# Four residual layers with chosen weights on one core: where the sync queue reads the ids

## The chip, the cores and the metric

The kernel runs on one core of a Trainium2 chip. The metric is the device time of one execution in microseconds (us), as the median of several runs. Five engines work side by side: TensorE (PE in the profile), VectorE (DVE), ScalarE (ACT), GpSimd (POOL) and SyncE (SP). SP computes nothing here. It waits, forms addresses and issues nearly all transfers, which 16 DMA engines then carry out.

## The reference, cut to what matters

Eight sequences of 128 tokens with 512 features pass through four layers, each added to its input. The layers choose weights by one id per sequence:

```python
def reference(x, itok_B_0_15, itok_B_0_7, itok_B_0_4, itok_B_2_6, ...):
    x = x + _L0_cond_ref(x, itok_B_0_15, L0_cond_weight)
    x = x + _L1_cond_ref(x, itok_B_0_7, L1_cond_W, L1_cond_Wr, L1_cond_A, L1_cond_B)
    x = x + _L2_cond_ref(x, L2_cond_weight, L2_cond_bias, L2_cond_lora_A, L2_cond_lora_B, itok_B_0_4)
    x = x + _L3_cond_ref(x, ..., itok_B_2_6, 0)
    return x

def _L0_cond_ref(x, adapter_ids, weight):
    w = weight[adapter_ids]                    # (8, 512, 512), one matrix for each sequence
    return jnp.einsum('bsi,boi->bso', x, w)
```

Layer 1 is a dense product with a router over eight small experts, to which a language id adds a bias. Layer 2 is a dense product with a low-rank part whose first factor is chosen by an id. Layer 3 is a gated feed-forward block of width 1376 with three low-rank parts, all chosen by an id. Everything is float32.

## The kernel before, in words

Each engine has a program of its own, written out by hand, and semaphores join them. There is no planner: the order of the work is the order of the lines in each engine's block.

**Layer 0** goes sequence by sequence (b = 0 to 7). Each sequence has its own 1 MB matrix, which SP fetches into a ring of three buffers (`w0_raw`, `W0_RING = 3`). The matrix of sequence 0 comes as four transfers of 256 KB (L367), and TensorE multiplies them directly as float32 (L1185). The matrix of every later sequence comes as three transfers of 512, 256 and 256 KB (L378). TensorE uses the first quarter directly (L1188). For the other three quarters ScalarE makes a rounded high part (L498, called at L533), VectorE the remainder (L749, called at L806), and TensorE takes three products of each (L1196 to L1198). ScalarE also copies the result of the sequence before out of PSUM (L510), TensorE transposes it (L1146), and VectorE adds it to x (L761). From sequence 3 on, TensorE also does layer 1's thin product with the router's weights (L1166).

**The sync queue** is the one that the change touches. In order of its lines it does this:

- It reads the eight ids of layer 0 into registers (L364). The helper `ids_of` (L356) does this with two instructions, both on L358: one reads the address of the array of ids, one reads the ids.
- It issues the four transfers of sequence 0 (L367).
- For b = 1 to 7 it issues x of the sequence (L371, from b = 2 on; x of sequences 0 and 1 is issued by ScalarE's queue), waits for a free buffer (L373, or L375 and L376 from b = 4 on) and issues the three transfers of the matrix (L378). Behind b = 2 it issues the router's weights and the language ids (L384, L385). Behind b = 3 (`b == W0_RING`) it reads the ids of layers 2 and 3 (L381, L382).
- It issues the weights of layer 1 (L388, four transfers, and L389).
- It waits until the splits of sequence 6 are done (L391, L392), then issues the weights of layer 2 (L393, and L395 with the ids of layer 2).
- It waits until layer 0 is done (L399, L400), then issues the masks and layer 3's first low-rank factors (L401, and L403 with the ids of layer 3), and later all else of layer 3.

The order around the change, in the code:

```python
if b > W0_RING:
    sp.wait_ge(w0_raw_used, b - W0_RING)
    sp.wait_ge(w0_lo, KC * (b - W0_RING))
```

Layers 1 to 3 work on halves of four sequences. Their products need no ids from SP other than through the transfers named above.

Of the kernel before, what the change touches and what calls it, by code (L numbers as in the profile page):

```python
# [37 lines left out]
B, S, D = 8, 128, 512  # L38
# [17 lines left out]
W0_RING = 3  # L56
# [5 lines left out]
def bass_four_residual_layers(nc, xT, ids0, ids1, ids2, ids3, w0, w1, aw1, b1, w2, a2, b2, bias2,  # L62
                              wgu, agu, sel, bgu, wd, ad, bd, out):
    ctx = ExitStack()
    with ctx:
# [188 lines left out]
        def x_f_tokens(o, cols):  # L254

            return x_f[:, cols.start // S:cols.stop // S, o]
# [51 lines left out]
        def chunks_of(n):  # L308

            return 2 * (n // 2) + 1, 2 * (n // 2) + 2  # L310

        def raw_slot(fc):
            return 0 if fc == 0 else (fc - 1) % 4 ^ 2
# [5 lines left out]
        def bgu_count(n, i):  # L319

            return 1 + 2 * n + i + 1
# [31 lines left out]

        @block.sync
        def _(sp):
            def ids_of(src, last):  # L356

                _, ids = nc.values_load_multi_w_load_instructions(  # L358
                    src[0:1, 0:B], engines=[mybir.EngineType.SP], min_val=0, max_val=last,
                    skip_runtime_bounds_check_because="each id only forms the DRAM address of a transfer, "  # L360
                                                      "and the transfer checks that address itself")
                return ids

            adapter0 = ids_of(ids0, w0.shape[0] - 1)  # L364

            for c in range(C):
                sp.dma_start(w0_raw[0][:, c], w0[adapter0[0]][:, c * D:(c + 1) * D]).then_inc(w0c_in[c], 16)  # L367
            for b in range(1, B):
                adapter = adapter0[b]
                if b >= 2:  # L370
                    sp.dma_start(x_f[:, b], xT[b]).then_inc(x_in[b], 16)  # L371
                if b == W0_RING:
                    sp.wait_ge(l0_tm, 1)  # L373
# [3 lines that stand above are left out]
                for k, (first, end) in enumerate(((0, 2), (2, 3), (3, 4))):  # L377
                    sp.dma_start(w0_raw[b % W0_RING][:, first:end],  # L378
                                 w0[adapter][:, first * D:end * D]).then_inc(w0_in[b % W0_RING][k], 16)
                if b == W0_RING:  # L380
                    adapter2 = ids_of(ids2, a2.shape[0] - 1)  # L381
                    adapter3 = ids_of(ids3, agu.shape[0] - 1)  # L382
                if b == 2:
                    sp.dma_start(aw1_raw[:], aw1).then_inc(aw1_in, 16)  # L384
                    sp.dma_start(lang_i[:], ids1.partition_broadcast(P)).then_inc(lang_in, 16)  # L385

            for o in range(C):
                sp.dma_start(w1_raw[:, o], w1[:, o]).then_inc(w1_in[o], 16)  # L388
            sp.dma_start(b1_raw[:], b1).then_inc(b1_in, 16)  # L389

            sp.wait_ge(w0_raw_used, 6)  # L391
            sp.wait_ge(w0_lo, KC * 6)  # L392
            sp.dma_start(w2_raw[:], w2).then_inc(w2_in, 16)  # L393
            for b in range(B):
                sp.dma_start(a2_raw[:, b], a2[adapter2[b]]).then_inc(a2_in, 16)  # L395
            sp.dma_start(b2_raw[:], b2).then_inc(b2_in, 16)
            sp.dma_start(bias_sb[:], bias2).then_inc(bias_in, 16)

            sp.wait_ge(l0_tm, 8)  # L399
            sp.wait_ge(l0_tr, 8)  # L400
            sp.dma_start(sel_raw[:], sel).then_inc(sel_in, 16)  # L401
            for b in range(B):
                sp.dma_start(agu_raw[:, b], agu[adapter3[b]]).then_inc(agu_in, 16)  # L403

            def load_wgu(fc):
                sp.dma_start(wgu_raw[raw_slot(fc)][:], wgu[fc]).then_inc(wgu_in[raw_slot(fc)], 16)

            def load_bgu(p):

                f1, f2 = chunks_of(2 * p)  # L410
                for b in range(B):
                    rows = slice(64 * (b % 2), 64 * (b % 2) + 64)
                    sp.dma_start(bgu_raw[rows, :, b // 2],  # L413
                                 bgu[adapter3[b], f1:f2 + 1].rearrange("f r n -> r f n")).then_inc(bgu_in, 16)

            sp.wait_ge(w12_lo, nth["w2_3"])
            load_wgu(0)
            for b in range(B):
                rows = slice(64 * (b % 2), 64 * (b % 2) + 64)
                sp.dma_start(bgu_raw[rows, 1, b // 2], bgu[adapter3[b], 0]).then_inc(bgu_in, 16)  # L420
            load_wgu(1)
            load_wgu(2)
            sp.wait_ge(l2_tm, 2)
            for b in range(B):
                sp.dma_start(ad_raw[:, b], ad[adapter3[b]]).then_inc(ad_in, 16)
            sp.wait_ge(wgu_lo, 1)
            sp.wait_ge(bgu_ready, 1)
            sp.wait_ge(main_done, 16)
            load_bgu(0)
            load_wgu(3)  # L430
            load_wgu(4)
            for p in range(1, PAIRS):
                sp.wait_ge(bgu_ready, bgu_count(2 * p - 1, 1))
                load_bgu(p)
                if p + 1 < PAIRS:
                    sp.wait_ge(wc_lo, 3 * 2 * p)
                    load_wgu(2 * p + 3)
                    load_wgu(2 * p + 4)
            sp.wait_ge(bgu_ready, bgu_count(2 * PAIRS - 1, 1))
            sp.wait_ge(wc_lo, 3 * 2 * PAIRS)  # L440
            for o in range(C):
                sp.dma_start(wd_raw[:, o], wd[o]).then_inc(wd_in[o], 16)
            sp.wait_ge(c22_ready, 2 * PAIRS)
            for b in range(B):
                rows = slice(64 * (b % 2), 64 * (b % 2) + 64)
                sp.dma_start(bd_raw[rows, b // 2], bd[adapter3[b]]).then_inc(bd_in, 16)
            for i, (o, cols) in enumerate(DOWN_PIECES):
                sp.wait_ge(x3_sum, i + 1)
                sp.dma_start(out[o, :, cols].rearrange("p (b s) -> p b s", s=S), x_f_tokens(o, cols)).then_inc(out_sent, 16)
            sp.wait_ge(out_sent, 16 * len(DOWN_PIECES))  # L450
# [1099 lines left out]
```

## Time and profile before

| | |
|---|---|
| median of 3 runs | 303.03 us (303.0 to 304.06) |
| the profiled execution's own time | 302.71 us |
| its span in the trace | 300.9 us |
| TensorE busy | 290.3 us, 96% of the span |
| VectorE, ScalarE, GpSimd busy | 204.4, 142.4 and 10.7 us |
| granted TensorE clock, mean | 0.997 |
| moved by DMA | 33.29 MB, 111 GB/s over the span |

The span is the time from the first to the last instruction of the program. The profiled execution took 1.8 us more than its span. A busy TensorE is not a TensorE at its peak, since the ends of its instructions are modelled and consecutive ones overlap. Times of rows are counted from the start of the span.

### The profile page before, as it was taken

How to read it: one execution, taken by the hardware profiler on the slowest of the kernel's cores; microseconds unless marked ns; L12 is line 12 of the kernel's file. 1: busy time of each engine (PE TensorE's matmuls, PEld its weight loads, DVE VectorE, ACT ScalarE, POOL GpSimd, SP SyncE). 2: the span in 40 equal slices, each digit the busy share in tenths (PEclk: the TensorE clock that was granted, in tenths of full speed). 3: DMA queues.
4: the chain of work that ended last, by engine and by line, in shares of the span. 5: the costliest groups of instructions: out<-in, count | busy, mean ns of one | idle time of the engine just before them, and what ended most of it. 6: DMA issues, size and time to landing. Idle time of an engine off the chain costs nothing.

```text
span 300.9 us, 4565 instructions
## 1 busy us (share of the span) xinstructions
PE 290.3 (96%) x1630; PEld 237.4 (79%) x1630; DVE 204.4 (68%) x378; ACT 142.4 (47%) x250; POOL 10.7 (4%) x25
## 2 busy tenths in 40 slices
PE   6799999999999999999999999999999999999995
PEld 5357788888888777787878878878889888888884
DVE  1297898894758899676967968878747959242003
ACT  2376861512425356756556465564633874211000
POOL 1030000000700001000000000000000000000000
PEclk9999999999999999999999999999999999999998
DMA  5989993004404062006116026031075200022004
GB/s 179 340 298 321 396 322 106 0 0 133 148 0 99 0 184 99 0 20 219 42 46 232 3 60 222 0 87 53 2 288 170 70 1 0 0 72 70 0 2 139
DMA packets 23255, 33.29 MB, mean 111 GB/s; under 512 B 2624, under 2 KB 15424, under 8 KB 23104
## 3 DMA queue, kind: packets, MB, share of 16 engines
q1 hardware_dynamic: 22944, 32.47, 32.5%
q10 hardware_dynamic: 288, 0.52, 0.6%
q8 instruction: 13, 0.21, 0.3%
q14 instruction: 10, 0.08, 0.1%
HBM read 30.89 MB, written 2.10 MB: 110 GB/s over the span
## 4 chain that ended last, share of the span: by engine, by line
PE 64%; DVE 13%; SPq 7%; DMA 6%; issue 4%; ACT 4%; DVEq 0%; ACTq 0%
PE bank L1212 11%; PE bank L1213 11%; PE bank L1214 11%; PE bank L1342 6%; PE bank L1343 6%; PE bank L1344 6%; DMA w_raw<-in_w 4%; SPq L413 3%; SPq L358 3%; DMA bgu_raw<-in_bgu 2%; PE bank L1321 2%; PE bank L1166 2%; DVE bgu_st L924 2%; DVE part L1038 2%; PE bank L1416 2%
## 5 line engine op out<-in xcount | busy, mean ns | idle before, releaser
L1212 PE MATMUL bank<-act_hl,wd_hl 128*128 128x512 f32 (+1 forms) x99 | 36.5, 369 | 0.0
L498 ACT ACTIVATE part<-bank 128x512 f32<-128x512 f32 x40 | 23.7, 595 | 26.8 <-PE bank L1344 26.2
L1213 PE MATMUL bank<-act_hl,wd_hl 128*128 128x512 f32 (+1 forms) x99 | 36.3, 367 | 0.0
L1214 PE MATMUL bank<-act_hl,wd_hl 128*128 128x512 f32 (+1 forms) x99 | 36.2, 365 | 0.0
L1038 DVE TENSOR_TENSOR part<-bank,part 128x512 f32<-128x512 f32 x40 | 26.7, 685 | 5.1 <-PE bank L1321 3.8
L749 DVE TENSOR_TENSOR w_hl<-w_raw,w_hl 128x512 fp32r<-128x512 f32 x29 | 19.3, 695 | 10.0 <-ACT w_hl L498 10.0
L924 DVE SCALAR_TENSOR_TENSOR bgu_st<-bgu_st,lo_rows,bgu_raw 128x512 fp32r<-128x512 f32 (+1 forms) x21 | 15.4, 773 | 14.3 <-ACT bgu_st L498 14.3
L749 DVE TENSOR_TENSOR act_hl<-act_f,act_hl 128x512 fp32r<-128x512 f32 x22 | 14.9, 689 | 12.9 <-ACT act_hl L498 12.8
L498 ACT ACTIVATE act_hl<-act_f 128x512 fp32r<-128x512 f32 x22 | 13.6, 624 | 20.8 <-PE bank L1214 18.8
L498 ACT ACTIVATE w_hl<-w_raw 128x512 fp32r<-128x512 f32 x29 | 17.8, 625 | 11.4 <-DMA w_raw<-in_w 10.0
L1214 PEld LDWEIGHTS bank<-act_hl,wd_hl 128*128 128x128 f32 x99 | 18.6, 188 | 3.1
L1212 PEld LDWEIGHTS bank<-act_hl,wd_hl 128*128 128x128 f32 x99 | 18.7, 189 | 3.0 <-issue 0.2
L1213 PEld LDWEIGHTS bank<-act_hl,wd_hl 128*128 128x128 f32 x99 | 18.7, 189 | 2.7
L664 ACT ACTIVATE act_f<-part 128x512 f32<-128x512 f32 x20 | 12.5, 632 | 15.7 <-DVE part L1038 15.7
L1072 DVE TENSOR_TENSOR x_f<-bank,x_f 128x512 f32<-128x512 f32 (+1 forms) x9 | 5.5, 629 | 19.5 <-PE bank L1437 19.5
L498 ACT ACTIVATE xb<-x_f 128x512 fp32r<-128x512 f32 x16 | 10.0, 628 | 17.3 <-DVE x_f L869 13.2
L1321 PEld LDWEIGHTS bank<-t_st,bgu_st 128*128 128x128 f32 x88 | 14.7, 188 | 3.9 <-DVE t_st L1022 0.9
L1321 PE MATMUL bank<-t_st,bgu_st 128*128 128x256 f32 x88 | 15.8, 284 | 0.9 <-DVE t_st L1022 0.9
L1344 PE MATMUL bank<-xb,wc_gate 128*128 128x512 f32 x40 | 15.7, 394 | 0.0
L1343 PE MATMUL bank<-xb,wc_gate 128*128 128x512 f32 x40 | 15.7, 392 | 0.0
L1342 PE MATMUL bank<-xb,wc_up 128*128 128x512 f32 x40 | 15.6, 391 | 0.0
L1343 PE MATMUL bank<-xb,wc_up 128*128 128x512 f32 x40 | 15.6, 390 | 0.0
(172 smaller groups left out, 689.9 us busy)
## 6 DMA issues: line engine op xcount, KB each, us to landing
w_raw<-in_w SPq DMA_DIRECT2D x22, 256.0 KB, 7.3
wgu_raw<-in_wgu SPq DMA_DIRECT2D x11, 512.0 KB, 4.5
bgu_raw<-in_bgu SPq DMA_DIRECT2D x40, 128.0 KB, 2.7
w_raw<-in_w SPq DMA_DIRECT2D x7, 512.0 KB, 7.2
wd_raw<-in_wd SPq DMA_DIRECT2D x4, 704.0 KB, 6.0
out<-x_f SPq DMA_DIRECT2D x7, 256.0 KB, 2.4
x_f<-in_xT SPq DMA_DIRECT2D x6, 256.0 KB, 7.1
w_raw<-in_w SPq DMA_DIRECT2D x1, 1024.0 KB, 6.6
```

The lines of the kernel that those rows point to most:

```text
L498: return act.activation(dst, src, ACT.Copy)
L664: act.activation(act_f[:, fc, h * HT:(h + 1) * HT], part[0][C_PART[k]][:], ACT.Silu).then_inc(silu_done, 1)
L749: return dve.tensor_tensor(dst, src, hi.bitcast(F32), ALU.subtract)
L924: return dve.scalar_tensor_tensor(out=st, in0=st.bitcast(F32), scalar=lo_rows16[:, 0:1], in1=raw, op0=ALU.mult, op1=ALU.add)
L1038: dve.tensor_tensor(dst[:], bank[4 * (n % 2) + b][:], dst[:], ALU.add).then_inc(c_added, 1)
L1212: pe.matmul(dst, w_hi, x[0][:, cols], start=start, stop=False)
L1213: pe.matmul(dst, w_hi, x[1][:, cols], start=False, stop=False)
L1214: return pe.matmul(dst, w_lo, x[0][:, cols], start=False, stop=stop)
L1321: ins = pe.matmul(dst[:, q * 2 * S:(q + 1) * 2 * S], bgu_st[fc % 2][:, pair, g], t3_st[:, g, pair * 2 * S:(pair + 1) * 2 * S], start=False ...
L1342: pe.matmul(dst[:], hi, x[0][c], start=(start and c == 0), stop=False, skip_group_check=True)
L1343: pe.matmul(dst[:], hi, x[1][c], start=False, stop=False, skip_group_check=True)
L1344: ins = pe.matmul(dst[:], lo, x[0][c], start=False, stop=(stop and c == 1), skip_group_check=True)
```

## The change

The sync queue reads the id of sequence 0 alone, issues the four transfers of sequence 0, and then reads the other seven ids of layer 0 with a second call of the helper. The reads of the ids of layers 2 and 3 move from behind the transfers of sequence 3 to behind the last transfers of layer 1. Nothing else differs.

```diff
-            def ids_of(src, last):
+            def ids_of(src, last, first=0, end=B):
 
                 _, ids = nc.values_load_multi_w_load_instructions(
-                    src[0:1, 0:B], engines=[mybir.EngineType.SP], min_val=0, max_val=last,
+                    src[0:1, first:end], engines=[mybir.EngineType.SP], min_val=0, max_val=last,
...
-            adapter0 = ids_of(ids0, w0.shape[0] - 1)
-
+            adapter0 = ids_of(ids0, w0.shape[0] - 1, 0, 1)
             for c in range(C):
                 sp.dma_start(w0_raw[0][:, c], w0[adapter0[0]][:, c * D:(c + 1) * D]).then_inc(w0c_in[c], 16)
+            adapter0 = [*adapter0, *ids_of(ids0, w0.shape[0] - 1, 1, B)]
             for b in range(1, B):
...
-                if b == W0_RING:
-                    adapter2 = ids_of(ids2, a2.shape[0] - 1)
-                    adapter3 = ids_of(ids3, agu.shape[0] - 1)
                 if b == 2:
...
             sp.dma_start(b1_raw[:], b1).then_inc(b1_in, 16)
+            adapter2 = ids_of(ids2, a2.shape[0] - 1)
+            adapter3 = ids_of(ids3, agu.shape[0] - 1)
```

## Rows read from the trace of the kernel before

**Rows 1.** The page's fourth part: shares of the chain that ended last, by line.

```profile
PE bank L1212 11%; PE bank L1213 11%; PE bank L1214 11%; PE bank L1342 6%; PE bank L1343 6%; PE bank L1344 6%; DMA w_raw<-in_w 4%; SPq L413 3%; SPq L358 3%; DMA bgu_raw<-in_bgu 2%; PE bank L1321 2%; PE bank L1166 2%; DVE bgu_st L924 2%; DVE part L1038 2%; PE bank L1416 2%
```

**Rows 2.** Waits of TensorE from 31.6 to 89 us: in total, times, longest.

```profile
PE bank L1196 <- DVE w_hl L749: 0.2, 1, 0.2
```

**Rows 3.** Timeline, all engines: start, us, what, idle before and what ended it.

```profile
12.01 1.30 ACT L498 ACTIVATE w_hl<-w_raw 128x512 fp32r<-128x512 f32 x2 [7.37 <-DMA w_raw<-in_w]
...
15.30 1.31 ACT L498 ACTIVATE w_hl<-w_raw 128x512 fp32r<-128x512 f32 x2 [0.44 <-DMA w_raw<-in_w]
...
25.16 1.02 PE L1188 MATMUL bank<-w_raw,x_f 128*128 128x512 f32 x2
...
25.97 0.63 ACT L498 ACTIVATE w_hl<-w_raw 128x512 fp32r<-128x512 f32 x1 [0.97 <-DMA w_raw<-in_w]
...
31.53 0.47 PE L1196 MATMUL bank<-w_hl,xa 128*128 128x512 f32 x1 [0.23 <-DVE w_hl L749]
```

**Rows 4.** The chain in order of time, 0 to 26 us: start, us, what.

```profile
0.73 0.86 SPq L358
1.62 1.49 SPq L358
...
10.71 1.14 PE bank L1185 x2
...
13.43 2.88 SPq L358
16.34 1.06 SPq L358
...
18.29 0.90 SPq L358
...
20.34 5.61 DMA w_raw<-in_w
```

**Rows 5.** Timeline of the sync queue, 0 to 42 us: start, us, what, count.

```profile
3.31 2.01 SPq L367 DMA_DIRECT2D w_raw<-in_w  x4
5.50 1.37 SPq L378 DMA_DIRECT2D w_raw<-in_w  x3
...
12.00 1.38 SPq L378 DMA_DIRECT2D w_raw<-in_w  x3
...
32.57 0.43 SPq L389 DMA_DIRECT2D b_raw<-in_b  x1
36.92 0.33 SPq L393 DMA_DIRECT2D w_raw<-in_w  x1
37.43 3.96 SPq L395 DMA_DIRECT2D a_raw<-in_a  x8
```

**Rows 6.** L378 from 5.4 to 7 us, sequence 1, from issue to landing.

```profile
DMA to landing us min/median/max: 6.5/6.6/6.8
```

**Rows 7.** Stretches: us, busy and count of PE, PEld, DVE, ACT, POOL; clock, DMA share, GB/s.

```profile
7.50:10.00 2.50, 2.16 (x6) 0.72 (x4) 0.00 (x0) 0.00 (x0) 0.00 (x0) 1.00 1.00 233
...
22.50:25.00 2.50, 2.50 (x17) 2.24 (x16) 2.22 (x4) 1.37 (x3) 0.00 (x0) 1.00 0.86 225
...
30.00:40.00 10.00, 9.77 (x52) 7.32 (x50) 9.15 (x18) 8.03 (x16) 0.00 (x0) 1.00 1.04 400
...
296.40:300.90 4.50, 0.88 (x8) 0.68 (x6) 1.34 (x3) 0.00 (x0) 0.00 (x0) 0.83 0.77 218
```

**Rows 8.** L378 from 12 to 13.4 us, sequence 3, from issue to landing.

```profile
DMA to landing us min/median/max: 8.0/8.1/8.2
```

**Rows 9.** L367, the four transfers of sequence 0, from issue to landing.

```profile
DMA to landing us min/median/max: 3.4/3.6/5.7
```

**Rows 10.** L378 from 19.5 to 21.2 us, sequence 4, from issue to landing.

```profile
DMA to landing us min/median/max: 4.5/5.6/6.2
```

**Rows 11.** Waits of the sync queue: in total, times, longest.

```profile
SPq L400 <- PE bank L1146: 3.7, 1, 3.7
```

**Rows 12.** Timeline of ScalarE from 34 to 62 us: layer 2's low-rank factors are split.

```profile
52.69 1.05 ACT L498 ACTIVATE a_hl<-a_raw 128x1024 fp32r<-128x1024 f32 x1
```

## The prediction

> **What bounds the kernel now.** I read the chain that ended last first. It is mostly TensorE, with 3% on L358, the reads of ids on the sync queue, and 4% on the transfers of `w_raw` [rows 1]. So the ids do stand on the path, and the question is where. Next I asked whom TensorE waits for. From 31.6 to 89 us it waits 0.2 us in all [rows 2]. Whatever moves the first split product of sequence 5, at 31.53 [rows 3], therefore moves everything behind it by the same amount, and what happens to SP later counts only if it is late by more than its cover. The case is decided before 31.53.
>
> In that stretch the chain passes the reads of ids twice [rows 4]. At the start these are 0.86 us for the address of the array and 1.49 us for eight ids. From 13.43 to 19.19 they are the two calls for layers 2 and 3: 2.88, 1.06, a second address, and 0.90 us, 5.8 us together. Behind them SP issues x and the matrix of sequence 4. Its second piece is issued at 20.34 and lands 5.61 us later, at 25.95 [rows 4], and ScalarE starts on it at 25.97 after 0.97 us of waiting [rows 3]. TensorE had no wait in front of its first product of sequence 4 at 25.16 [rows 3]. So these 0.97 us are what the stall of 5.8 us costs; the rest of it was covered by transfers already under way.
>
> Sequences 1 and 2 are bound by transfers as well. ScalarE starts on sequence 1 at 12.01 after waiting 7.37 us [rows 3]. The first piece was issued at 5.50 and took 6.5 us, so it landed at 12.0 [rows 5, 6]. For sequence 2 it waits too, at 15.30 [rows 3]. Once the queue is full the DMA engines move 400 GB/s [rows 7], 256 KB in 0.66 us. So what delays the first piece of sequence 1 delays sequences 1, 2 and 3 as a block.
>
> **Part 1: one id instead of eight at the start.** Two reads remain. Reading eight ids took 1.49, 1.06 and 0.90 us, reading an address 0.86 us [rows 4]. The spread at eight ids is as large as the distance to the address, so I see mostly a fixed time. The gain is between 0 and 1.49 - 0.86 = 0.63 us. I take 1.49 - 1.06 = 0.43. The transfers of sequence 0 then go out at 2.9 instead of 3.31 [rows 5]. For sequence 0 itself that is worthless: its last product ends at 11.85 [rows 4], and the next matrix is not there before 12.0. It counts because sequence 1 is issued behind it.
>
> The Trainium skill (Runtime: NRT & Kernel Launch, Instruction fetch mechanics) says that a read of registers costs about 200 ns for each register, even in bulk. By it the first read would shrink by 1.4 us. The trace speaks against it: eight ids took 0.90 us [rows 4], less than eight times 0.2.
>
> **Part 2: a second call in front of sequence 1.** This is the cost. SP now reads an address and seven ids between the last transfer of sequence 0 and the first of sequence 1. For the ids I take 1.06, between 0.90 and 1.49. The address is the open term. It took 0.86 us on an idle queue, but 2.88 right behind three issued transfers [rows 4]. That row is nearest in kind, but there the queue was full, and its transfers took 8.0 to 8.2 us to land [rows 8]; here at most four are under way, which land in 3.4 to 3.6 [rows 9]. I take the middle, 1.87, and keep both ends. With 0.07 us between instructions the call costs 1.87 + 1.06 + 0.07 = 3.0 us, between 1.8 and 4.0. The first piece of sequence 1 is issued at 5.50 - 0.43 + 3.0 = 8.1. It finds a nearly empty queue. There 256 KB landed in 3.4 us [rows 9], so 512 KB need 3.4 + 0.66 = 4.1, and the like piece of sequence 4, on a short queue, took 4.5 [rows 10]. With 4.3 it lands at 12.4, against 12.0 before: **0.4 us later**, though issued 2.6 us later, because before it stood in a queue. Behind the second call on SP stand x and the matrix of sequence 2, the router's weights, the language ids, and x and the matrix of sequence 3, thirteen transfers in all with sequence 1. All are issued later, but they land as one stream, 0.66 us for 256 KB behind sequence 1, and so shift by the same 0.4.
>
> **Part 3: the two calls leave their place behind sequence 3.** x of sequence 4 is issued right behind sequence 3's last piece, and its matrix as soon as the splits of sequence 1 free the buffer, about when ScalarE goes on to sequence 2 at 15.30 [rows 3]. The stream then runs on. The last piece of sequence 3, issued at about 13.1, landed 8.2 us later, at 21.3 [rows 5, 8]. x is 0.66 us behind it and the second piece of sequence 4 another 1.97, so it lands at 23.9 + 0.4 = 24.3, before ScalarE wants it at 25.0 + 0.4. The wait of 0.97 us goes: **1.0 us gained**. What is late next is TensorE itself, so I give no more. Below, the bound is 0: from 22.5 to 25 us the transfers ran at 225 GB/s [rows 7], and this may come again.
>
> **Part 4: the calls in their new place.** SP is through with layer 1's transfers at 33.0 and issues the next at 36.92 [rows 5]; between them it waits 3.9 us for the splits of sequence 6. The two calls take 5.8 us there if the address costs 2.88 again. So layer 2's weights go out 1.9 us late. SP's next wait, 3.7 us at L400 [rows 11], absorbs that before layer 3's factors. Layer 2's low-rank factors were issued by 41.4 [rows 5]; even 1.9 us later and with 8.2 us to land [rows 8] they are there at 51.5, and ScalarE splits them at 52.69 [rows 12]. The cost is nothing; if that cover were gone, up to 1.9 us.
>
> **The sum.** 0.4 - 1.0 = -0.6 us. Against the profiled execution (span 300.9 us and 1.8 around it, own time 302.7) that is 302.1. The median of the runs stands 0.3 above that execution, so 302.4 on its scale. A measurement of this kernel can tell about 0.5%, 1.5 us, from no change; by that bound this is the same.
>
> **Rivals.** *The second call is cheap* (chance 0.22). The address costs 0.86 us, as at the start, and the ids 0.90, so sequence 1 is issued at 5.50 - 0.43 + 1.8 = 6.9 and lands at 11.0 to 11.4, 0.6 to 1.0 us sooner than before. With part 3: -1.6 to -2.0 us, 301.2. For it: the queue is short. Against it: the only read behind transfers took 2.88 [rows 4].
>
> *Slower: the transfers of sequence 1 start late and slowly* (0.20). The place is ScalarE's wait for sequence 1. The call costs 4.0 us, the issue is at 9.1 to 9.5. And a queue that starts anew has a slow stretch: from 7.5 to 10 us, 4 us behind the first issue, the DMA engines were fully busy at 233 GB/s [rows 7], and one piece of sequence 0 took 5.7 us where the others took 3.4 to 3.6 [rows 9]; the restart at 19.2 has the same from 22.5 on [rows 7]. If 2 us of this strike sequence 1, its first piece lands at 9.3 + 4.3 + 2 = 15.6, 3.6 late, less 1.0: +2.6 us, 305.6; with half the slow stretch 304.6. The rival decides once the landing is later than 12.0 + 1.0 + 1.5 = 14.5.
>
> A second price may stand on top. Sequence 0's last piece would land 3.6 us after 4.6, and TensorE would be done at 9.3 and idle to 14 or later. In the stretches with work the granted clock is 1.00, the full 2.4 GHz; in the last one, where TensorE runs out of work, it is 0.83 [rows 7], so part of it at 1.2 GHz. If that happens here, a sequence's work, which fits into the 6.4 us from 25.16 to 31.53 [rows 3], could take some 3 us more, an estimate, in part hidden by the waits for sequences 2 and 3. The Trainium skill (TensorE: Matmul & The Clock Gate, Part 1) says that an idle engine is put back to the half clock and must work before it gets the full one again. That rule speaks against this change, and the tail of this trace agrees with it.
>
> *Nothing is won at sequence 4* (0.12). The slow stretch at 22.5 us belongs to that matrix and not to the restart, its second piece stays late, and the sum is +0.4: 303.4.
>
> *The time of a read goes with the number of ids* (0.04). One id saves 0.63 us, seven cost 1.06: -0.8 us, 302.2. By the Trainium skill (Runtime: NRT & Kernel Launch, Instruction fetch mechanics) one id would save 1.4 us and seven cost 1.4, a sum of -1.2 and 301.8. That the change does not do what it says can be so only in this: the first read is no shorter, +0.43 us, within the forecast's own range.
>
> **How the numbers follow.** The forecast has 0.42, its own range 301.6 to 303.5. The range that holds the time 8 times in 10 takes in the cheap call down to 300.9 and the slow case up to 305.0. Faster by over 1.5 us: the cheap call and an edge of the forecast, 0.27. Slower by over 1.5: 0.20. Within: 0.53.
>
> **What would show it.** In the profile after: two pairs of L358 in front of 10 us, the second 3.0 us long (1.8 if cheap, 4.0 if slow); L378 for sequence 1 issued at 8.1; ScalarE's first split of a matrix at 12.4; no wait of ScalarE at sequence 4's second piece; L393 issued some 2 us later than before, and nobody waiting for it; the first L1196 of sequence 5 at 30.9 instead of 31.53, and TensorE without waits behind it. The prediction is wrong if that instruction moves by more than 1.5 us, or if TensorE waits behind it where it did not before.

## The result and the profile after

The changed kernel takes 305.14 us (median of 22 runs), the kernel before 303.18 us over the same runs. The ratio is **1.0067, interval 1.0049 to 1.0084**: slower by 2.0 us, just outside the range that I gave, and on the other side of the forecast of -0.6 us. The profiled execution took 304.02 us with a span of 302.2, against 302.71 and 300.9: 1.3 us more. It is the quickest of the 22, and a second profile of the same kernel (e8, below) comes closer to the typical run.

The page, first the busy time of TensorE and then the chain that ended last by engine:

```profile
PE 289.9 (96%) x1630; PEld 237.1 (78%) x1630; DVE 204.5 (68%) x378; ACT 142.4 (47%) x250; POOL 10.7 (4%) x25
...
PE 73%; DVE 10%; SPq 5%; ACT 4%; DMA 3%; issue 3%; DVEq 0%; ACTq 0%
```

TensorE works as long as before; the added time is waiting. The reads of ids in the chain in order of time (start, us, what), which answer to [rows 4]:

```profile
0.73 0.87 SPq L358
1.62 0.80 SPq L358
...
4.67 1.18 SPq L358
5.89 0.06 SPq L358
5.97 3.21 SPq L358
```

One id is read in 0.80 us where eight took 1.49. The second call has an instruction more, which forms the address of the second id (0.06), and its read of seven ids takes **3.21 us**. The call lasts from 4.67 to 9.18, 4.5 us. The timeline of the sync queue shows what comes of it (as [rows 5]):

```profile
2.62 2.01 SPq L366 DMA_DIRECT2D w_raw<-in_w  x4
9.35 1.37 SPq L378 DMA_DIRECT2D w_raw<-in_w  x3
...
11.38 1.36 SPq L378 DMA_DIRECT2D w_raw<-in_w  x3
...
16.92 1.37 SPq L378 DMA_DIRECT2D w_raw<-in_w  x3
...
32.95 0.43 SPq L386 DMA_DIRECT2D b_raw<-in_b  x1
38.28 0.33 SPq L392 DMA_DIRECT2D w_raw<-in_w  x1
```

Sequence 0 goes out 0.7 us sooner, sequence 1 at 9.35 instead of 5.50. Sequence 4 (16.92 instead of 19.82) is early, as the move of the two later calls wanted. Issue to landing of sequence 1 and of sequence 2, from L378 in two stretches:

```profile
DMA to landing us min/median/max: 3.7/4.3/4.5
...
DMA to landing us min/median/max: 6.2/6.4/6.5
```

So sequence 1's first piece lands at 13.0 (12.0 before), and sequence 2's, issued 2.0 us behind it, at 17.6 (15.3 before). At full speed they would be 3.3 us apart (three pieces of 0.66 and one of 1.31); they are 4.6 apart. What waits, from the timeline of all engines (as [rows 3]):

```profile
13.04 0.63 ACT L497 ACTIVATE w_hl<-w_raw 128x512 fp32r<-128x512 f32 x1 [8.54 <-DMA w_raw<-in_w]
13.15 1.10 PE L1187 MATMUL bank<-w_raw,x_f 128*128 128x512 f32 x2 [2.94 <-DMA w_raw<-in_w]
...
17.64 1.33 ACT L497 ACTIVATE w_hl<-w_raw 128x512 fp32r<-128x512 f32 x2 [1.25 <-DMA w_raw<-in_w]
...
22.02 1.30 ACT L497 ACTIVATE w_hl<-w_raw 128x512 fp32r<-128x512 f32 x2 [0.72 <-DMA w_raw<-in_w]
...
25.38 1.26 ACT L497 ACTIVATE w_hl<-w_raw 128x512 fp32r<-128x512 f32 x2
...
32.88 0.47 PE L1195 MATMUL bank<-w_hl,xa 128*128 128x512 f32 x1
```

ScalarE starts on sequence 1 at +1.0 us, on sequence 2 at +2.3, on sequence 3 at +2.0 (20.05 in the trace before). At sequence 4 it waits for no transfer any more, and the first split product of sequence 5 comes at 32.88 instead of 31.53, **+1.35 us**. From there to the end every instruction of VectorE keeps this distance within 0.4 us, the last with +1.33, and TensorE has no wait at all between 31 and 90 us.

The calls in their new place cost nothing. They run from 33.4 to 37.9, 4.5 us, and behind them SP still waits 0.3 us for the splits of sequence 6 (L391). So L392 goes out 1.4 us late because these splits are 1.35 us late, and not because of the calls. SP's next wait still lasts 3.5 us, and ScalarE splits layer 2's low-rank factors at +1.33, like all else (waits of SP, then the timeline of ScalarE, as [rows 11, 12]):

```profile
SPq L399 <- PE bank L1145: 3.5, 1, 3.5
...
SPq L391 <- DVE w_hl L748: 0.3, 1, 0.3
```

```profile
54.02 1.05 ACT L497 ACTIVATE a_hl<-a_raw 128x1024 fp32r<-128x1024 f32 x1
```

### The profile page after: what moved, and what is told of

Read it like the earlier page. It is cut to its first block, busy times and chain, and to the rows that moved or that the text cites. A ratio compares the mean times of both kernels' runs of the same rounds, so it can differ in the third digit from the quotient of the medians.

```text
span 302.2 us, 4568 instructions
## 1 busy us (share of the span) xinstructions
PE 289.9 (96%) x1630; PEld 237.1 (78%) x1630; DVE 204.5 (68%) x378; ACT 142.4 (47%) x250; POOL 10.7 (4%) x25
## 4 chain that ended last, share of the span: by engine, by line
PE 73%; DVE 10%; SPq 5%; ACT 4%; DMA 3%; issue 3%; DVEq 0%; ACTq 0%
PE bank L1211 11%; PE bank L1212 11%; PE bank L1213 11%; PE bank L1341 8%; PE bank L1342 8%; PE bank L1343 8%; PE bank L1320 3%; PE bank L1165 3%; DMA w_raw<-in_w 2%; SPq L358 2%; PE bank L1415 2%; SPq L412 2%; DMA bgu_raw<-in_bgu 1%; PE bank L1195 1%; PE bank L1258 1%
## 5 line engine op out<-in xcount | busy, mean ns | idle before, releaser
L497 ACT ACTIVATE w_hl<-w_raw 128x512 fp32r<-128x512 f32 x29 | 17.7, 623 | 11.3 <-DMA w_raw<-in_w 11.0
L663 ACT ACTIVATE act_f<-part 128x512 f32<-128x512 f32 x20 | 12.5, 632 | 15.6 <-DVE part L1037 15.6
L1071 DVE TENSOR_TENSOR x_f<-bank,x_f 128x512 f32<-128x512 f32 (+1 forms) x9 | 5.5, 628 | 19.5 <-PE bank L1436 19.5
```

The costliest lines, as they stand in the source:

```text
L497: return act.activation(dst, src, ACT.Copy)
L663: act.activation(act_f[:, fc, h * HT:(h + 1) * HT], part[0][C_PART[k]][:], ACT.Silu).then_inc(silu_done, 1)
```

## The experiments

The theory after the result: the second call is what costs, and most of its excess is one slow read. Three things had to be told apart: move against split, what makes the read slow, and what the clock does in TensorE's gap of 3 us. All ratios are to the kernel before. "Sequence 5" is the time of its first split product in the one profiled execution of each run, 31.53 before.

| run | ratio, interval | second call, us | sequence 5 |
|---|---|---|---|
| changed kernel | 1.0067, 1.0049 to 1.0084 | 4.5 | 32.88 |
| e8, the same again | 1.0063, 1.0041 to 1.0085 | 4.4 | 33.72 |
| e1, move only | 0.9972, 0.995 to 0.9993 | none | 31.31 |
| e11, the same again | 0.998, 0.996 to 1.0 | none | 30.97 |
| e2, split only | 1.0078, 1.0047 to 1.0108 | 4.5 | 33.76 |
| e3, second call reads all eight | 0.9979, 0.996 to 0.9998 | 2.5 | 31.74 |
| e4, second call first of all | 1.0078, 1.0051 to 1.0105 | 3.8 | 34.75 |
| e6, gap of TensorE filled | 1.0058, 1.0036 to 1.008 | 4.6 | 33.93 |
| e7, second call behind sequence 1 | 1.0037, 1.0014 to 1.0059 | 3.8 | 32.69 |
| e10, ScalarE issues sequence 1 | 0.9998, 0.997 to 1.0025 | 4.1 | 30.83 |

**e1, the move alone.** Sequence 0 to 7's ids are read in one call again:

```diff
-            adapter0 = ids_of(ids0, w0.shape[0] - 1, 0, 1)
+            adapter0 = ids_of(ids0, w0.shape[0] - 1)
...
-            adapter0 = [*adapter0, *ids_of(ids0, w0.shape[0] - 1, 1, B)]
```

> Sequence 0 to 7's ids are read in one call at the start as before; only the calls for layers 2 and 3 stand in their new place. Theory (the loss is the second call in front of sequence 1, the move alone gains): about 1.0 us faster than the kernel before, ratio 0.997, the first split product of sequence 5 at 30.5 against 31.53. Rival (the move gains nothing, the slow stretch of transfers at sequence 4 comes again): ratio 1.000, that instruction within 0.3 us of 31.5. Second rival (the calls are late in their new place and cost there): slower, ratio 1.003 or more, and TensorE waits in layer 1 or 2.

Measured 302.07 us against 303.26, ratio 0.9972: the theory's case, and the second rival falls. The first rival's sign at sequence 5 did come, 31.31 instead of 30.5, so the trace has to say why. Timeline of e1, then its stretches (columns as [rows 7]):

```profile
12.79 1.30 ACT L496 ACTIVATE w_hl<-w_raw 128x512 fp32r<-128x512 f32 x2 [8.26 <-DMA w_raw<-in_w]
...
31.31 0.47 PE L1194 MATMUL bank<-w_hl,xa 128*128 128x512 f32 x1
```

```profile
7.50:10.00 2.50, 2.50 (x4) 0.97 (x3) 0.00 (x0) 0.00 (x0) 0.00 (x0) 1.00 0.95 208
...
22.50:25.00 2.50, 2.50 (x14) 2.07 (x14) 2.15 (x5) 2.21 (x5) 0.00 (x0) 1.00 1.05 398
```

In this execution sequence 1 came 0.8 us late by a slower start of the transfers (208 GB/s from 7.5 to 10), and sequence 5 still 0.2 early: the move gained 1.0. The stretch from 22.5 to 25 us, at 225 GB/s in [rows 7], now runs at 398. It had gone with the restart behind the stall, not with the matrix. That answers the first rival.

Here the price of the calls in their new place shows, too: SP no longer waits for the splits of sequence 6, the next transfer is issued at 37.90 instead of 36.92, and SP's wait behind it shrinks from 3.7 to 2.5 us. That is about 1 us late, and hidden.

**e2, the split alone.** The other half; the two later calls go back behind sequence 3:

```diff
+                if b == W0_RING:
+                    adapter2 = ids_of(ids2, a2.shape[0] - 1)
+                    adapter3 = ids_of(ids3, agu.shape[0] - 1)
...
-            adapter2 = ids_of(ids2, a2.shape[0] - 1)
-            adapter3 = ids_of(ids3, agu.shape[0] - 1)
```

> One id first, a second call for the other seven in front of sequence 1, and the calls for layers 2 and 3 behind sequence 3 as before. Theory (two stalls on the sync queue instead of one, the transfers run dry twice): slower than the kernel before by 3 us or more, ratio 1.010, and slower than the changed kernel by about 1. Rival (the second stall is hidden because TensorE is late already): as the changed kernel, ratio 1.007.

Measured 305.56 us, ratio 1.0078. That lies between the theory's 1.010 and the rival's 1.007, and the medians alone don't decide. The stretches and the timeline do:

```profile
22.50:25.00 2.50, 1.73 (x5) 0.87 (x6) 2.27 (x4) 2.12 (x4) 0.00 (x0) 1.00 0.88 252
25.00:27.50 2.50, 2.50 (x17) 2.15 (x16) 2.32 (x4) 1.08 (x3) 0.00 (x0) 1.00 0.94 227
```

```profile
27.55 1.35 ACT L498 ACTIVATE w_hl<-w_raw 128x512 fp32r<-128x512 f32 x2 [1.47 <-DMA w_raw<-in_w]
```

The slow stretch behind the second stall is there again, and ScalarE waits 1.47 us for sequence 4. But the wait is not all loss: sequence 3 comes 2.8 us late (22.87) and sequence 5 2.2 us late (33.76), no later than in e8, the second profile of the changed kernel (33.72). The intervals of the two kernels overlap. So the second stall leaves its marks in the trace, and what it adds to the time is somewhere between nothing and the 1 us of the theory; these runs do not decide it.

**e3 and e4, what makes the read slow.** e3 reads all eight ids in the second call, from the start of the array. e4 puts the second call in front of the transfers of sequence 0.

```diff
-            adapter0 = [*adapter0, *ids_of(ids0, w0.shape[0] - 1, 1, B)]
+            adapter0 = ids_of(ids0, w0.shape[0] - 1)
```

```diff
             adapter0 = ids_of(ids0, w0.shape[0] - 1, 0, 1)
+            adapter0 = [*adapter0, *ids_of(ids0, w0.shape[0] - 1, 1, B)]
             for c in range(C):
                 sp.dma_start(w0_raw[0][:, c], w0[adapter0[0]][:, c * D:(c + 1) * D]).then_inc(w0c_in[c], 16)
-            adapter0 = [*adapter0, *ids_of(ids0, w0.shape[0] - 1, 1, B)]
```

> As the changed kernel, but the second call reads all eight ids from the start of the array. Theory A (the second read is slow, 3.2 us, since it begins at the second id): it takes 0.9 to 1.5 us, sequence 1 is issued about 2 us sooner than in the changed kernel, at 7.3, and the ratio to the kernel before is 1.000. Theory B (it is slow since it stands behind four issued transfers): again 3 us or so for one of the two reads, and the ratio is that of the changed kernel, 1.007.

> As the changed kernel, but the second call stands in front of the transfers of sequence 0, so no transfer of the sync queue is ahead of it. Theory A (where it begins makes the read slow): the read of the seven ids takes 3 us, sequence 0 is issued at 6.7, slower than the kernel before by about 2.5 us. Theory B (the transfers ahead make it slow): both reads take about 0.9 us, sequence 0 is issued at 4.5, 1.2 us later than before, ratio to the kernel before 1.000 to 1.003.

The reads of the second call in the chain of e3, then in that of e4:

```profile
4.67 1.58 SPq L358
6.28 0.89 SPq L358
```

```profile
2.43 0.98 SPq L358
3.44 0.06 SPq L358
3.53 2.71 SPq L358
```

Theory A holds in both. Eight ids from the start take 0.89 us behind the same four transfers where seven from the second id took 3.21, and these seven take 2.71 with no transfer of SP's ahead. e3 does more reading than the changed kernel and is 2.4 us quicker (302.77 us). e4's ratio of 1.0078 is worth 2.4 us, as theory A had it; its trace shows 3.2 at sequence 5, since its own start of the transfers was slow too. Transfers ahead are not without effect: the address took 0.98 us in e4 and 1.12 to 1.75 behind the four transfers of sequence 0 in seven traces.

e3 shows a second thing, in ScalarE's starts on sequences 1 and 2:

```profile
11.32 0.63 ACT L497 ACTIVATE w_hl<-w_raw 128x512 fp32r<-128x512 f32 x1 [6.80 <-DMA w_raw<-in_w]
...
16.38 1.30 ACT L497 ACTIVATE w_hl<-w_raw 128x512 fp32r<-128x512 f32 x2 [0.79 <-DMA w_raw<-in_w]
```

Sequence 1 is 0.7 us sooner than before the change and sequence 2 is 1.1 us later. So even with a short call the stream behind sequence 1 does not follow it.

**e5 and e9, the shapes of a read.** e5 added eight calls whose ids nobody uses:

```diff
+            for first, end in ((0, 1), (0, 7), (0, 8), (1, 2), (1, 8), (2, 8), (4, 8), (1, 3)):
+                ids_of(ids0, w0.shape[0] - 1, first, end)
```

> The changed kernel with eight more calls of the helper, whose ids nobody uses, on the idle sync queue behind the transfers of layer 3's last factor: ids 0 to 0, 0 to 6, 0 to 7, 1 alone, 1 to 7, 2 to 7, 4 to 7, 1 to 2, in this order. Theory (a read that doesn't begin on an even place of the array fetches its ids one by one, about 0.4 us each): 0.9 us for those that begin at 0, 0.9 for 1 alone, 2.7 to 3.2 for 1 to 7, 0.9 for 2 to 7 and 4 to 7, and about 1.2 for 1 to 2. Rival (the number of ids decides, eight is special): 0 to 6 takes as long as 1 to 7, 3 us. Second rival (any start behind the first id is slow, whatever the number): 1 alone, 2 to 7 and 4 to 7 take 3 us as well. The time is the changed kernel's, ratio 1.007.

It told nothing of the shapes: none of the eight calls left an instruction in the trace. Its own second call took 1.12 + 3.07 us, and its single execution 305.35 us, as the changed kernel. e9 makes the move alone and uses the ids:

```diff
             for b in range(B):
+                first, end = ((0, 1), (1, 2), (0, 8), (1, 8), (2, 8), (4, 8), (0, 7), (6, 8))[b]
+                chosen = ids_of(ids3, agu.shape[0] - 1, first, end)[b - first]
                 rows = slice(64 * (b % 2), 64 * (b % 2) + 64)
-                sp.dma_start(bd_raw[rows, b // 2], bd[adapter3[b]]).then_inc(bd_in, 16)
+                sp.dma_start(bd_raw[rows, b // 2], bd[chosen]).then_inc(bd_in, 16)
```

> The move alone, and in front of each of the eight transfers of layer 3's last factor, late on an otherwise quiet sync queue, one more call of the helper whose id that transfer uses: ids 0 to 0, 1 alone, 0 to 7, 1 to 7, 2 to 7, 4 to 7, 0 to 6, 6 to 7, in this order. Theory (the start of the read decides, at an odd place ids are fetched one by one): 2.7 to 3.2 us for 1 to 7, about 0.9 for every other. Rival (the number decides: eight in one piece, seven one by one): 0 to 6 takes about as long as 1 to 7. Second rival (any start behind the first id is slow): 2 to 7 and 4 to 7 take 1.5 us or more. If all take 0.8 to 1.0 us, the slow read belongs to the start of the kernel. The total is that of the move alone within 1 us, since TensorE waits for this factor only at the end of the first half.

e9's single execution took 301.49 us, within 1 us of the move alone. L358 of e9 in eight stretches, one read of ids in each (ns min/median/max, start), in the order of the edit:

```profile
L358 SPq TENSOR_LOAD <-in_ids x1: 455/455/455, 228.5 to 228.5; - x1
L358 SPq TENSOR_LOAD <-in_ids x1: 465/465/465, 230.8 to 230.8; - x1
L358 SPq TENSOR_LOAD <-in_ids x1: 879/879/879, 233.0 to 233.0; - x1
L358 SPq TENSOR_LOAD <-in_ids x1: 2887/2887/2887, 235.6 to 235.6; - x1
L358 SPq TENSOR_LOAD <-in_ids x1: 2550/2550/2550, 240.2 to 240.2; - x1
L358 SPq TENSOR_LOAD <-in_ids x1: 486/486/486, 244.5 to 244.5; - x1
L358 SPq TENSOR_LOAD <-in_ids x1: 1641/1641/1641, 246.7 to 246.7; - x1
L358 SPq TENSOR_LOAD <-in_ids x1: 827/827/827, 250.1 to 250.1; - x1
```

All three of my theories were too simple. Counted in steps of 0.41 to 0.49 us, the reads are 1, 1, 2, 7, 6, 1, 4 and 2 steps. That fits one rule: from a start at a multiple of four, ids are fetched four at a time, and every other id by itself. Ids 0 to 7 are two fours, 4 to 7 one; 0 to 6 are a four and three single ones; 1 to 7 are seven and 2 to 7 six single ones. The rule was made after the numbers, from one execution of each shape, and no run tests it on a new one. But seven from the second id, read behind sequence 0, took 2.78 to 3.21 us in five traces (the changed kernel, e2, e5, e6 and e8). Eight from the first vary more than e3 alone would say: 0.88 to 1.85 us in most places, but 2.29 and 2.45 us behind the weights of layer 1 in e6 and e1, and 2.37 in e10.

**e7, the second call behind sequence 1.** Two ids first, then seven transfers, then eight ids:

```diff
-            adapter0 = ids_of(ids0, w0.shape[0] - 1, 0, 1)
+            adapter0 = ids_of(ids0, w0.shape[0] - 1, 0, 2)
...
-            adapter0 = [*adapter0, *ids_of(ids0, w0.shape[0] - 1, 1, B)]
             for b in range(1, B):
+                if b == 2:
+                    adapter0 = ids_of(ids0, w0.shape[0] - 1)
```

> The changed kernel, but the first call reads ids 0 and 1, the transfers of sequences 0 and 1 are issued behind it, and the second call stands in front of sequence 2 and reads all eight ids from the start of the array. Theory (the second call costs only where the queue runs dry behind it): no gap between the transfers of sequences 0 and 1, sequence 1 issued at 4.8 to 5.5, the second call hidden; as good as the move alone (0.9972) or 0.5 us better, ratio 0.996. Rival (any call among the first transfers costs): ratio 0.999 or more.

Measured 303.89 us, ratio 1.0037: the rival's case. The timeline of e7:

```profile
16.65 1.27 ACT L498 ACTIVATE w_hl<-w_raw 128x512 fp32r<-128x512 f32 x2 [1.42 <-DMA w_raw<-in_w]
...
22.30 1.10 PE L1188 MATMUL bank<-w_raw,x_f 128*128 128x512 f32 x2 [1.38 <-DMA w_raw<-in_w]
```

Here the address took 2.38 us and the ids 1.39, and x of sequence 2 was issued at 10.67. The last of the seven transfers landed at 13.7, x at 14.3 and sequence 2's first piece at 16.6, 1.3 us later than before the change. So there was no gap in front of x, but the pieces behind it came slowly, at 287 GB/s from 12.5 to 15 us and 304 from 15 to 17.5. The seven transfers, 2 MB, lasted 6.9 us from the start of the call (6.83), and the call together with x's way took 3.8 + 3.6 = 7.4. That a fuller queue would have kept the full rate is an inference; no run shows it. And the two ids at the start took 1.42 us where eight take 1.49, so nothing was gained there either.

**e6 and e8, the clock.** e8 is the changed kernel again. e6 adds twelve products that fill TensorE's gap:

```diff
                 ins.then_inc(l0_tm, 1)
+                if b == 0:
+                    for _ in range(12):
+                        pe.matmul(bank[7][:, 0:P], ident[:], ident[:], start=True, stop=True)
```

> The changed kernel once more, to compare with the two above on the same chip and to see its reads of ids in a second execution: ratio 1.007; the read of ids 1 to 7 takes 2.7 to 3.3 us again. If it takes 1.5 or less, the reads vary by chance and the theory of the start falls.

> The changed kernel with twelve more products of the identity on TensorE behind sequence 0, 2.7 us of work in the 3.5 us in which it waits for sequence 1. Theory (in part of the runs the clock falls in this gap, which costs about 0.6 us of the median): 0.6 us faster than the changed kernel, ratio to the kernel before 1.005, granted clock 1.00. Rival (the clock plays no part in the medians): ratio 1.007 as before. If the products get in the way of sequence 1: slower, 1.008 or more.

Stretches of e8 and then of e6:

```profile
12.50:15.00 2.50, 1.35 (x3) 0.58 (x4) 0.80 (x2) 1.38 (x3) 0.00 (x0) 0.97 0.84 279
15.00:17.50 2.50, 2.50 (x9) 2.01 (x9) 0.94 (x2) 1.33 (x3) 0.00 (x0) 0.50 0.96 318
```

```profile
12.50:15.00 2.50, 1.77 (x8) 0.81 (x7) 0.69 (x1) 1.14 (x2) 0.00 (x0) 1.00 0.87 281
15.00:17.50 2.50, 2.05 (x10) 1.11 (x9) 0.94 (x2) 1.58 (x4) 0.00 (x0) 1.00 0.93 309
```

In e8 TensorE had waited 3.12 us and then ran at 0.50 of its clock, 1.2 GHz, through most of sequence 1. In e6 it stays at 2.4. The times are the same: 304.99 and 305.0 us. The first 22 runs of the changed kernel say so too: the ten with a mean granted clock of 0.997 or more have a median of 305.14 us, the twelve below it 305.17. While sequence 2's transfers arrive at 280 to 320 GB/s, TensorE has time to be slow. The clock does fall, and costs nothing that can be measured. What the two have in common against the first profile is that slow transfer: ScalarE starts on sequence 2 at 18.57 and 18.74 instead of 17.64, and at 18.63 in e5. That is the likely reason why the typical run of the changed kernel costs 2 us and the first profiled one only 1.3.

**e10 and e11.** e11 is e1 again. e10 cuts the start further: SP reads one id, issues sequence 0 and then reads all eight, while ScalarE's queue reads two ids and issues sequence 1.

```diff
+            _, first_two = nc.values_load_multi_w_load_instructions(
+                ids0[0:1, 0:2], engines=[mybir.EngineType.Activation], min_val=0, max_val=w0.shape[0] - 1,
...
+            for k, (first, end) in enumerate(((0, 2), (2, 3), (3, 4))):
+                act.dma_start(w0_raw[1][:, first:end],
+                              w0[first_two[1]][:, first * D:end * D]).then_inc(w0_in[1][k], 16)
```

> The move alone, with the start cut further: the sync queue reads id 0 alone, issues sequence 0, then reads all eight; ScalarE's queue reads ids 0 and 1 for itself and issues the transfers of sequence 1. Theory (only a dry queue costs, and the sync queue's second call now stands beside transfers of sequences 0 and 1): transfers start at 2.6 as in the changed kernel and do not run dry, 0.5 us faster than the move alone, ratio 0.995. Rival (the two queues share the DMA engines, sequence 1 lands no sooner, and sequence 2 stands behind the second call): ratio 0.998 or more.

> The move alone once more, beside the one above: ratio 0.997. If it comes out at 1.000 or more, its gain was chance.

The rival's case again: 302.98 us, 0.9998, while e11 gives 302.03 us and 0.998. Two rows of e10 show where the gain goes, one of its second read of ids and one of TensorE at the last piece of sequence 0:

```profile
6.46 2.37 SPq L358
```

```profile
12.04 1.13 PE L1191 MATMUL bank<-w_raw,x_f 128*128 128x512 f32 x2 [1.23 <-DMA w_raw<-in_w]
```

The read took 2.37 us although it begins at the first id; here transfers of two queues are under way. Sequence 1, issued 1.4 us sooner, lands at 11.3 instead of 12.4, but sequence 0's last piece, now under way beside it, takes 7.7 us to land instead of 6.1 and is multiplied only at 12.04 (11.09 in e11), and TensorE begins sequence 1 at 13.00 instead of 12.50. Sequence 3 lands at 19.6 instead of 20.5, but the first split product of sequence 5 is only 0.14 us ahead of e11's.

This profile is one of e10's quick executions (302.05 us). The runs scatter (301.1 to 304.4), and in two groups: the six with a mean granted clock of 0.997 or more have a median of 302.1 us, the six at 0.994 one of 303.6; none of e11's twelve is below 0.998. Whether the clock makes them longer or late transfers make both is not shown. The move alone stays the best kernel of the study, and e3 (0.9979) can't be told from it.

## Why the prediction was wrong

**What bounds the kernel** held. The case is decided before sequence 5, the shift there is the shift at the end, and TensorE shows no new wait behind it.

**Part 1** held in direction and was a little larger: 0.69 us instead of 0.43, just above its upper bound of 0.63. Its reason, "mostly a fixed time", holds only in part: on a quiet queue one id takes 0.46 us and eight take 0.88.

**Part 2 failed, twice.** First in the size of a term. I wrote "For the ids I take 1.06, between 0.90 and 1.49"; they took 3.21. The whole call was 4.5 us against 3.0, outside its upper bound of 4.0. I had put the doubt on the wrong read: the address, which I called the open term, took 1.18 us, and the ids, which I called known, made the excess. Every row that I had for a read of ids began at the first id and took eight. Seven from the second was a form that the trace before had never shown, and I priced it as the form that it had shown. e9 says what separates them. The rival that lets the time go with the number of ids would not have caught it: it priced seven ids at the same 1.06, and in e9 eight ids take 0.88 us and six take 2.55. Of the 1.5 us by which the call was longer, 0.6 arrived at sequence 1 (13.0 instead of the 12.4 that I forecast), since part 1 gave 0.3 more and the landing took 3.7 us instead of 4.3.

Second in "they land as one stream ... and so shift by the same 0.4". Sequence 1 came 1.0 late, sequence 2 2.3, sequence 3 2.0; in e8 sequences 2 and 3 came 3.3 and 3.2 late. In these traces the transfers behind a queue that has run dry came at 208 to 346 GB/s between 10 and 17.5 us (the changed kernel, e2, e5, e6 and e8), and that struck sequence 1's later pieces and sequence 2. This is the larger failure of the two: by sequence 3 it adds 1.0 us in the first profile and 2.0 in e8 to sequence 1's own delay. It is there with a short call as well: in e3 sequence 1 was 0.7 us early and sequence 2 1.1 us late.

**Part 3** held: e1 and e11 gain 1.0 and 0.9 us on their own start of sequence 1, and e8 falls from +3.2 at sequence 3 to +2.2 at sequence 5. In the first profile it is 0.6.

**Part 4** held in what it says of the cost, which is nothing. In the first profile the two calls took 4.5 us instead of 5.8 and ended 0.3 us before the splits that SP waits for; in e1 they made layer 2's weights about 1 us late, and SP's next wait absorbed it.

**The sum** by what was measured, from the two profiles of the changed kernel: +2.0 to +3.2 at sequence 3, -0.6 to -1.0 from the move, +1.35 to +2.2. The median says +2.0.

**The slower rival** was the right one, with the right two causes: a call of 4 us and the slow stretch. Its chance of 0.20 was too low for a mechanism with both its rows in hand, and its point of decision was misplaced. I had it decide on the landing of sequence 1's first piece after 14.5; that piece landed at 13.0, and the loss came in the pieces behind it. Its second price, the clock, was real in the records and free in the time. That the read of the seven ids was slow because of the transfers ahead is refuted as the main cause by e3 and e4; that transfers lengthen a read is seen in e10. The cheap call did not happen either, and would have been worth little: in e3, with a call of 2.5 us, ScalarE starts on sequence 1 at 11.32, inside the 11.0 to 11.4 of that rival, and the time is 302.77 us and not 301.2, no better than the move alone.

Left open is why transfers run well below 400 GB/s for some time after a queue has started. Every trace here has such a stretch in its first 17 us, and one behind 20 us only where SP stood still for 5.8 us behind sequence 3 (the kernel before and e2). But a dry queue is not all of it: e9, in which SP made no second call there, fell to 308 GB/s from 15 to 17.5 us, and ScalarE waited once for a single late piece at sequence 5 in e6 (1.52 us) and at sequence 6 in e8 (0.79 us).

## What to carry to other kernels

A new instruction form has no row in the trace before, however much it looks like its neighbour: bound it by its worst decomposition (here one fetch for each id), not by the neighbour's spread. Read ids from a start at a multiple of four and in fours; reading one more that nobody needs was three times quicker here (0.88 against 2.89 us). Put a stall of the sync queue where what is already queued lasts longer than the stall and the next transfer's way to landing together; seven transfers in front of a call of 3.8 us were not enough (e7), and how many would be is not shown. Otherwise leave the reads together in front. And do not take the delay of the first transfer for the delay of the stream: look at the transfers behind it.

## What the runs showed of the hardware

A read of ids into registers on e9's quiet queue took 0.46 us for one and 0.49 us for four from a multiple of four, 0.88 for eight from the start, and 2.55 and 2.89 for six and seven that begin elsewhere. For each register that is 0.41 to 0.47 us where ids go singly and 0.11 to 0.12 in fours. The Trainium skill (DMA: Bandwidth & Descriptors, Latency and other measured facts) gives a floor of about 600 ns for such a read and says that the compiler unrolls it by four. The measured floor is lower, 0.46 us. Steps of four ids are in the measured times, but each read is one instruction in the trace, so no run shows that they are that unrolling.

TensorE's granted clock fell to 0.50, 1.2 GHz, in the work behind waits of 4.6 us in e4, 3.1 in e8, 3.2 in e2 and 2.9 in e5, and not behind the 2.9 us in the first profile of the changed kernel. In e4 it was at 0.50 from 10 to 15 us, in sequence 0.

Eight ids from the first of an array took 1.49 us as the first read of the program in the kernel before, e1, e9 and e11, 0.88 us on e9's quiet queue, and up to 2.45 us with transfers under way (e1, behind layer 1's weights).
